# Attention by pairs of heads: values and output projection for two heads at once, low parts in place

## The reference

```
mod = (silu(c) @ wmod).reshape(4, 6, 1, 512)         # shift, scale, gate, twice
h = layernorm(x) * (1 + ca) + sa                     # x: 4 x 512 x 512
q = h @ Wq.T            # 32 heads of 128, rope
k, c_kv = rope part of h @ Wkr.T, h @ Wdk.T          # 8 key/value heads, 4 query heads share one
k, v = c_kv @ Wupk.T, c_kv @ Wupv.T
attn = softmax(causal(q k.T * scale))                # per batch and head, 512 x 512
x = x + ga * ((attn v) @ Wo.T)
h = layernorm(x) * (1 + cb) + sb
w = top8 of softmax(h @ router.T + bias), dense      # 64 experts, each only a bias vector
x = x + gb * (h * sum(w) + w @ expert_bias)
```

## Time and profile before

| what | us |
|---|---|
| median of 3 runs (1528.67 to 1531.39) | 1531.01 |
| the profiled execution | 1527.11 |
| its span | 1525.8 |
| TensorE busy | 1481.6 (97%) |
| VectorE busy | 1167.2 (76%) |
| GpSimd busy | 1079.0 (71%) |
| ScalarE busy | 973.3 (64%) |

### The profile page before, as it was taken

The page is one execution under the profiler, slowest core; times in us unless marked ns, Lnnn a source line. Parts: engine busy times, 40 slices in busy tenths (PEclk is TensorE's granted clock), DMA queues, the critical chain, the costliest instruction groups (busy, mean ns, idle before and its releaser), DMA issues.

```text
span 1525.8 us, 24881 instructions
## 1 busy us (share of the span) xinstructions
PE 1481.6 (97%) x7474; PEld 1264.1 (83%) x7474; DVE 1167.2 (76%) x3441; ACT 973.3 (64%) x2317; POOL 1079.0 (71%) x827
## 2 busy tenths in 40 slices
PE   8979999999999999999999999999999999999976
PEld 4668888888888888888888888888888888888865
DVE  6866777777777777777777777777888899897766
ACT  3356767676676766667666776767566666666663
POOL 1667767676676767767667676766678888886765
PEclk9999999999999999999999999999999999999997
DMA  8547665666656666666666665667778888888750
GB/s 308 211 149 226 203 198 189 207 193 201 197 197 197 197 196 202 203 179 208 199 197 209 201 194 175 215 200 212 220 250 261 260 266 278 268 253 269 247 181 28
DMA packets 210982, 322.03 MB, mean 211 GB/s; under 512 B 38416, under 2 KB 128272, under 8 KB 210848
## 3 DMA queue, kind: packets, MB, share of 16 engines
q1 hardware_dynamic: 210528, 320.33, 66.4%
q10 hardware_dynamic: 320, 0.11, 0.0%
HBM read 179.42 MB, written 140.94 MB: 210 GB/s over the span
## 4 chain that ended last, share of the span: by engine, by line
PE 86%; DVE 5%; POOL 3%; issue 2%; ACT 1%; DMA 1%; SPq 0%; DVEq 0%; POOLq 0%; ACTq 0%
PE bank_s L489 22%; PE bank_o L588 21%; PE bank_pv L573 15%; PE bank_s L538 14%; PE bank_s L512 6%; PE bank_s L500 5%; PE bank_s L468 1%; DMA wmod<-in_wmod 1%; PE bank_o L436 1%; POOL PT_lo L1458 1%; PE bank_s L606 1%; DVE y L1058 1%; DMA blocks<-blocks 0%; POOL rot_c L1446 0%; DVE h_raw L1070 0%
## 5 line engine op out<-in xcount | busy, mean ns | idle before, releaser
L1458 POOL TENSOR_TENSOR PT_lo<-PT_raw,PT_hi 128x640 fp32r<-128x640 f32 x252 | 407.0, 1638 | 91.2 <-ACT PT_hi L839 91.1
L825 ACT ACTIVATE probs<-probs,row_inv 128x512 f32<-128x512 f32 (+3 forms) x512 | 258.8, 554 | 200.5 <-DVE row_inv L1128 200.5
L1446 POOL TENSOR_TENSOR rot_c<-rot_c,rot_s 128x512 f32<-128x512 f32 x128 | 165.7, 1294 | 197.0 <-DVE rot_s L1091 196.8
L818 ACT ACTIVATE probs<-probs,row_min 128x512 f32<-128x512 f32 (+3 forms) x512 | 280.4, 551 | 7.8 <-DVE row_min L1122 7.8
L1451 POOL TENSOR_TENSOR qT_lo<-rot_c,qT_hi 128x512 fp32r<-128x512 f32 x128 | 167.2, 1306 | 92.8 <-ACT qT_hi L800 92.8
L1122 DVE CUSTOM_DVE_ANT_0 probs<-bank_s,mask 128x512 f32<-128x512 f32 (+3 forms) x512 | 231.2, 487 | 1.0 <-issue 0.6
L489 PE MATMUL bank_s<-hT_lo,wq_hi 128*128 128x512 f32 x500 | 205.3, 411 | 5.4 <-issue 3.7
L1145 DVE STREAM_TRANSPOSE blocks<-probs 128x384 f32<-128x384 f32 x508 | 205.2, 442 | 4.1 <-POOL hT_lo L1436 2.1
L588 PE MATMUL bank_o<-wo_lo,OT_hi 128*128 128x512 f32 x504 | 196.7, 390 | 4.2 <-DVE OT_lo L1153 4.2
L588 PE MATMUL bank_o<-wo_hi,OT_lo 128*128 128x512 f32 x504 | 196.5, 390 | 0.0
L588 PE MATMUL bank_o<-wo_hi,OT_hi 128*128 128x512 f32 x504 | 196.3, 390 | 0.0
(11 more groups left out here) (252 smaller groups left out, 3397.6 us busy)
## 6 DMA issues: line engine op xcount, KB each, us to landing
blocks<-blocks SPq DMA_DIRECT2D x127, 640.0 KB, 4.6
PT_raw<-blocks SPq DMA_DIRECT2D x504, 160.0 KB, 3.1
stage<-in_wq SPq DMA_DIRECT2D x32, 256.0 KB, 4.0
vblocks<-kv_raw SPq DMA_DIRECT2D x32, 256.0 KB, 4.3
kv_raw<-vblocks SPq DMA_DIRECT2D x128, 64.0 KB, 2.6
stage<-in_wo SPq DMA_DIRECT2D x32, 256.0 KB, 3.8
split_wq<-wq_hi SPq DMA_DIRECT2D x32, 256.0 KB, 3.6
split_wq<-wq_lo SPq DMA_DIRECT2D x32, 256.0 KB, 3.9
```

Source lines behind the costliest of these rows:

```text
L818: ins = act.activation(row(t, qt), row(t, qt), ACT.Exp, bias=row_min[m][:, qt:qt + 1], scale=-1.0, accum_out=row_sum[m][:, qt:qt + 1])
L825: ins = act.activation(row(t, qt), row(t, qt), ACT.Copy, scale=row_inv[t % 2][:, qt:qt + 1])
L1446: pool.tensor_tensor(rot_c[:], rot_c[:], rot_s[:], ALU.add).then_inc(pool_a, 1)
L1458: pool.tensor_tensor(lo[:, at], raw_of(t)[:, at], hi[:, at].bitcast(F32), ALU.subtract).then_inc(pool_t, 1)
```

## The change

Two heads, `2p` and `2p+1`, form a pair `p`. Their transposed probabilities lie side by side in buffers of twice the size, and one matmul takes columns of both: first the upper two tiles of queries (2 and 3), with key tiles 0 to 3, then the lower two (0 and 1), with key tiles 0 and 1. The output projection goes by pair too, upper tiles in the next odd step and lower tiles in the even step behind it. `PT_raw` and `PT_lo` are one buffer: GpSimd subtracts in place. There is one buffer of values for two. The key and value projections move to `h` = 1 and `h` = 3, the feed-forward pieces to even steps, the weight pieces `wo` one step later. The transposed loads of both heads of a pair are issued in the odd step, when the lower values of the pair before are done. The last two heads go singly as before.

```
-CHUNK_STEP = {0: [0], 1: [1], 2: [2], 3: [3], 5: [4], ...}
+CHUNK_STEP = {1: [0], 2: [1], 3: [2], 4: [3], 5: [4], ...}
-FFN_FROM = (AGAIN - SHARED + 1) * GROUP + 3
+PAIRS = (ALL - 2) // 2
+UPPER, LOWER = (2, 3), (0, 1)
+FFN_FROM = (AGAIN - SHARED + 1) * GROUP + 4
-        PT_hi = whole.take("PT_hi", [P, CAUSAL], F32R)
-        PT = [PT_hi, whole.take("PT_lo", [P, CAUSAL], F32R)]
-        PT_raw = whole.take("PT_raw", [P, CAUSAL])
+        PT_hi = whole.take("PT_hi", [P, 2 * CAUSAL], F32R)
+        PT_raw = Region(whole.at).take("PT_raw", [P, 2 * CAUSAL])
+        PT = [PT_hi, whole.take("PT_lo", [P, 2 * CAUSAL], F32R)]
-        v = [[whole.take(f"v_{p}{i}", [P, QT, HD], F32R) for p in ("hi", "lo")] for i in range(2)]
+        v = [whole.take(f"v_{p}", [P, QT, HD], F32R) for p in ("hi", "lo")]
+        def pair_done(p, tiles):
+            return 2 * p + (1 if tiles == UPPER else 2)
             def scores(...):
-                    if qt == 2 and h == 2 and u + 1 < UNITS:
+                    if qt == 2 and h == 3 and u + 1 < UNITS:
                         pe.wait_ge(dve_kr, u + 2)
-                    if qt == 2 and h == 0 and u > 0:
+                    if qt == 2 and h == 1 and u > 0:
                         pe.wait_ge(dve_vt, u + 1)
+            def values_pair(p, tiles):
+                t = 2 * p
+                pe.wait_ge(pool_t, 2 * (t + 1) + 2)
+                if t % GROUP == 0:
+                    pe.wait_ge(dve_v, t // GROUP + 1)
+                if pair_done(p, tiles) > 1:
+                    pe.wait_ge(dve_o, pair_done(p, tiles) - 1)
+                to = bank["pv"][:].rearrange("p (i k) -> p i k", i=2 * SUBS)
+                last_key = tiles[-1]
+                for kb in range(last_key + 1):
+                    first = max(kb, tiles[0])
+                    at = KEY_OFFSET[kb] // SUBS + (first - kb) * SUB
+                    size = (last_key + 1 - first) * SUB
+                    for n, (a, w) in enumerate(passes(v, PT)):
+                        ps = w[:].rearrange("p (i k) -> p i k", i=2 * SUBS)[:, :, at:at + size]
+                        mm = pe.matmul(to[:, :, (first - tiles[0]) * SUB:], a[:, kb, :], ps, ...)
+                mm.then_inc(pe_pv, 1)
+            def out_pair(p, tiles):
+                pe.wait_ge(dve_o, pair_done(p, tiles))
...
+                for j in tiles:
+                    for h in heads:
+                        o_at = (2 * (j - tiles[0]) + h % 2) * P
+                        for n, (o, w) in enumerate(passes(OT, wo)):
+                            mm = pe.matmul(bank[f"o{j}"][:], o[:, o_at:o_at + P], w[:, h, :], ...)
             def step(t):                                   # TensorE
                 scores(t + 1, QUERY_ORDER, before, n)
+                if h % 2 == 1 and t > 1:
+                    values_pair(t // 2 - 1, LOWER)
                 if t + 3 < ALL:
                     q_proj(t + 3)
-                if h == 0 and u + 1 < UNITS:
+                if h == 1 and u + 1 < UNITS:
                     k_proj(u + 1)
-                if h == 2 and u + 1 < UNITS:
+                if h == 3 and u + 1 < UNITS:
                     v_proj(u + 1)
-                if t >= 2:
-                    out_head(t - 2)
+                if h % 2 == 1 and t > 1:
+                    out_pair(t // 2 - 1, UPPER)
+                if h % 2 == 0 and t > 2:
+                    out_pair(t // 2 - 2, LOWER)
...
-                if 0 < t < ALL - 2:
-                    values(t - 1)
+                if h % 2 == 0 and t > 0:
+                    values_pair(t // 2 - 1, UPPER)
             def step(t):                                   # ScalarE
-                if t >= 2:
-                    o_split_hi(t - 2)
-                if 0 < t < ALL - 2:
+                if h % 2 == 1 and t > 1:
+                    pair_split_hi(t // 2 - 1, UPPER)
+                if h % 2 == 0 and t > 2:
+                    pair_split_hi(t // 2 - 2, LOWER)
+                if h % 2 == 0 and 0 < t < ALL - 2:
                     split_moved_hi(t - 1)
-                if h == 0:
-                    v_split_hi(u)
...
+                if h == 1:
+                    v_split_hi(u)
                 normalise(t + 1, 0)
                 normalise(t + 1, 1)
+                if h % 2 == 1:
+                    split_moved_hi(t - 1)
                 if t + 3 < ALL:
                     q_split(t + 3)
             def step(t):                                   # VectorE
+                if h % 2 == 1 and t > 1:
+                    pair_split_lo(t // 2 - 1, UPPER)
                 mask_and_max(t + 1, 0)
-                if t >= 2:
-                    o_split_lo(t - 2)
+                if h % 2 == 0 and t > 2:
+                    pair_split_lo(t // 2 - 2, LOWER)
                 mask_and_max(t + 1, 1)
...
                 if h == 2 and u > 0:
-                    add_out(u - 1, range(2, QT))
-                if h == 0:
-                    v_split_lo(u)
+                    add_out(u - 1, UPPER)
+                if h == 3 and u > 0:
+                    add_out(u - 1, LOWER)
                 invert_sums(t + 1, 0)
                 if t + 3 < ALL:
                     q_rope(t + 3)
                 invert_sums(t + 1, 1)
-                if h == 0 and u + 1 < UNITS:
+                if h == 1:
+                    v_split_lo(u)
+                if h % 2 == 1:
+                    transpose_blocks(t + 1, QUERY_ORDER[:2])
+                if h == 1 and u + 1 < UNITS:
                     k_rope(u + 1)
-                if h == 2 and u + 1 < UNITS:
+                if h == 3 and u + 1 < UNITS:
                     transpose_values(u + 1)
...
-                if moved(t + 1):
+                if h % 2 == 1:
+                    transpose_blocks(t + 1, QUERY_ORDER[2:])
+                elif moved(t + 1):
                     transpose_blocks(t + 1)
             def step(t):                                   # GpSimd
-                if t > 0:
+                if h % 2 == 0 and t > 0:
                     split_moved_lo(t - 1)
...
                 if t + 3 < ALL:
                     q_rope(t + 3)
+                if h % 2 == 1:
+                    split_moved_lo(t - 1)
+                if t + 3 < ALL:
                     q_split(t + 3)
-                if h == 0 and u + 1 < UNITS:
+                if h == 1 and u + 1 < UNITS:
                     k_rope(u + 1)
             def load_transposed(t):                        # SyncE
-                elif t > 0:
-                    sp.wait_ge(pool_t, 2 * t)
+                elif t > 1:
+                    sp.wait_ge(pe_pv, t // 2 * 2)
             for t in range(ALL):
-                if moved(t):
+                if t % 2 == 1 and moved(t):
+                    load_transposed(t - 1)
                     load_transposed(t)
```

More of the change, by code:

```diff
@@ L240, in build @@
         wdk = [wdk_hi, early.take("wdk_lo", [P, CH, HID], F32R)]
-        assert early.at <= probs_at
+        assert early.at <= blocks_at
         modrow = Region(probs_at).take("modrow", [BATCH, 2, HID])
[L243 to L253, removed]
+        under_blocks = Region(blocks_at)
+        h_raw = [under_blocks.take(f"h_raw{i}", [P, SEQ]) for i in range(2)]
+        c_in = under_blocks.take("c_in", [P, CH, BATCH])
+        c_exp = under_blocks.take("c_exp", [P, CH, BATCH])
+        c_silu = under_blocks.take("c_silu", [P, CH, BATCH])
+        stats = under_blocks.take("stats", [P, QT, 6])
+        mean_var = under_blocks.take("mean_var", [P, TILES, 2])
+        ve = under_blocks.take("ve", [P, TILES])
+        rstd = under_blocks.take("rstd", [P, TILES])
+        power = under_blocks.take("power", [P, TILES])
+        assert under_blocks.at <= probs_at
         assert whole.at <= nc.sbuf_usable_end
@@ L553, in transpose_part @@
                 mm.then_inc(pe_t, 1)
+            def values_pair(p, tiles):
[13 more added lines that the diff above has]
+                        ps = w[:].rearrange("p (i k) -> p i k", i=2 * SUBS)[:, :, at:at + size]
+                        mm = pe.matmul(to[:, :, (first - tiles[0]) * SUB:], a[:, kb, :], ps,
+                                       start=(kb == 0 and n == 0), stop=(kb == last_key and n == 2))
+                mm.then_inc(pe_pv, 1)
@@ new lines, in out_pair @@
+            def out_pair(p, tiles):
+                u = 2 * p // GROUP
+                heads = [2 * p % GROUP, 2 * p % GROUP + 1]
+                pe.wait_ge(dve_o, pair_done(p, tiles))
+                for h in heads:
+                    wait_weights(u, f"wo{h}")
+                if p == 0:
+                    pe.wait_ge(dve_vt, 1)
+                for j in tiles:
+                    if heads[0] == 0 and u > 0:
+                        pe.wait_ge(dve_y, added(u - 1, j))
+                    for h in heads:
+                        o_at = (2 * (j - tiles[0]) + h % 2) * P
+                        for n, (o, w) in enumerate(passes(OT, wo)):
+                            mm = pe.matmul(bank[f"o{j}"][:], o[:, o_at:o_at + P], w[:, h, :],
```

(18 more changed lines are left out.)

132 lines of the change are left out of this document (70 added, 62 removed).

## The result

| | before | after |
|---|---|---|
| median of 4 runs each, us | 1530.95 | 1595.63 |
| range of the runs | 1528.67 to 1531.39 | 1594.98 to 1597.17 |
| span of the profiled execution | 1525.8 | 1593.7 |
| score matmuls of step 4 (start-up ahead of it) | 142.85 | 143.99 |
| steps 4 to 91, 22 shared units | 938.87 (42.68 each) | 967.67 (43.99 each) |

The change makes the kernel slower: ratio 1.0427, interval 1.0409 to 1.0445. The rows of the table under the span are distances between the first score matmuls of steps, the last one from there to the end of the span, and their differences add up to the span's: 1.1 + 28.8 + 33.2 - 0.7 + 5.4 = 67.9 us.

The account below looks back on a forecast made before the run. TensorE, busy 97% of the span, was taken as the bound. Profiled 1527.1 us, plus 29 for 23 shared units and 28 for eight feed-forward units, each net of matmul time saved, made 1584; forecast 1585, range 1525 to 1618.

Parts of the forecast that it names:

- Matmul time removed: TensorE's values product: 18 matmuls a pair for 24, 3.42 us for 3.80, so 0.77 a unit and 24 us off.
- VectorE's chain: Head 1's odd step: key's rotation ends at 12.6, so scores of tile 2 stall TensorE 0.85 us a unit.
- the low part of the values, 1.12 or more: VectorE's new subtraction behind the reciprocal in head 1's odd step, taken as 1.12 us or more, ending at 9.3.
- GpSimd's chain: Second head's low part ends 8.5 us into head 2's even step, delaying upper values; with the rotation's wait 1.3 us.
- Head 2's lower values: Lower values due at 24.1 wait for VectorE, ending at 24.6 behind ScalarE's late copy, and start at 24.75: 0.65 us.
- Sum of a shared unit: Stalls 1.3 + 0.65 + 0.1 less 0.77 saved: +1.3 us, bounds -0.77 and +2; 23 units, +29 us.
- Feed-forward units: Eight units carrying feed-forward work: stalls of 4.3 us, net +3.5 a unit, 28 us in all; bounds +1.2 and +5.2.
- Cost nothing, with 1 us of cover: Transposed loads of a pair: first head lands at about 7.8, second at 9.5, wanted at 8.9 and 12.2.
- The end: The tail, where a pair's output work moves ahead of the last wait: nothing, bounds +-2.7 us.
- TensorE's 24 us come through whole: Faster rival: both chains, VectorE's rotation and GpSimd's low part, stay hidden, giving 1507 us; chance 0.14.
- Only the rotation waits: Rival: only the key's rotation stalls TensorE, GpSimd's chain being 1 us shorter: 6 us, 1535 (1528 to 1545); chance 0.15.
- Loads land late: Rival: paired loads come in bursts and delay GpSimd and the upper values; 1 us late is 63 us, 1648; chance 0.13.

Follow-up runs that it names:

- the by-head runs: Values' matmuls one head at a time, 36 a pair for 18: in the changed kernel 1624.58 us (ratio 1.0639), in the 1519.28 us version 1551.19 us (1.0139).
- The run with the rotation's wait taken away: Changed kernel with VectorE making the low part of the values ahead of the query's rope, not behind it: 1594.59 us, ratio 1.0436.
- the fastest version: Changed kernel with three orders mended, store behind loads, gating behind query's low part, GpSimd's statistics and VectorE's last feed-forward operation earlier: 1519.28 us, ratio 0.9936.
- the orders were mended: Changed kernel with VectorE's, GpSimd's and ScalarE's orders altered, SyncE's store behind the loads, and feed-forward operations of GpSimd and VectorE moved: 1519.28 us, ratio 0.9936.
- mending all: Changed kernel with low part of the values early, GpSimd's weight piece behind, and ScalarE's upper-values and feed-forward copies ahead, together: 1557.28 us, ratio 1.0184.

## Why the prediction was right, and where its terms were off

**The total and its sign.** 1595.6 for 1585, within 1525 to 1618, by the mechanism forecast: the removed matmul time is real, and waits in the written order of VectorE and GpSimd give back more. The range is wide and held a rival too. The 10.6 us over the forecast come from the feed-forward units and the end, not from the shared units.

**Matmul time removed: right.** 3.42 predicted; measured 2.42 and 1.10, of which 0.07 is the restart: 3.45. By the formula of the Trainium skill (TensorE: Matmul & The Clock Gate, "Back-to-back issue gap"), columns over the clock and 2.5 ns for each matmul, the by-head runs would be an estimated 3 us slower; they were about 30 slower. The prediction used this formula where it isn't meant: the section gives it for an isolated gap, and says that in a stream of weight loads and matmuls both set the spacing, with about 131 ns for 512 columns. That figure doesn't hold here either, as 512 columns took 227 ns.

**VectorE's chain: the mis-sized term.** The prediction let the key's rotation end at 12.6 and TensorE stall for 0.85, 0.95 with the restart. The rotation ended at 13.05 (694.23, the odd step having begun at 681.18); the tile started 1.24 late, and the scores as a whole took 1.58 more. The term at fault is "the low part of the values, 1.12 or more": it took 1.80, in each of the 22 shared units. A second, smaller term stood in no step of the walk: the query projection's wait for the mask, 0.22. The 1.12 came from one row; I did not ask what GpSimd did beside it. Here GpSimd's sum of the query's rope (689.28 to 690.57) starts 0.04 ahead of it; the subtraction ended at 691.12, 0.55 after the sum. Without a neighbour it takes 0.69, as the run with the subtraction ahead shows. The trace of the kernel before held the same: in 6 of its 22 shared units the subtraction took 1.84 or 1.85, as it met an instruction of GpSimd just begun. The row of 1.12 began 1.00 behind the start of one, and GpSimd's next one was then 0.45 longer:

```profile
743.49 1.85 DVE L1111 TENSOR_TENSOR v_lo<-kv_raw,v_hi 128x512 fp32r<-128x512 f32 x1
```
```profile
699.93 1.58 POOL L1458 TENSOR_TENSOR PT_lo<-PT_raw,PT_hi 128x640 fp32r<-128x640 f32 x1
701.46 2.03 POOL L1458 TENSOR_TENSOR PT_lo<-PT_raw,PT_hi 128x640 fp32r<-128x640 f32 x1
...
743.22 1.58 POOL L1458 TENSOR_TENSOR PT_lo<-PT_raw,PT_hi 128x640 fp32r<-128x640 f32 x1
```

The Trainium skill (SBUF — State Buffer, "Who interferes with whom") states the rule that I should have used: a VectorE instruction with two SBUF inputs and a GpSimd instruction that reads SBUF exclude each other, and the later one waits. The trace agrees: 1.80 us in the 31 places beside GpSimd's sum, 0.69 in the one place without it. The low part of the output (L1231), which reads one of its inputs from PSUM, kept its 0.69 beside GpSimd.

**GpSimd's chain: exact, and hidden.** 8.5 into the even step predicted, 8.51 measured. But the stall before it was larger than forecast, so TensorE came at 8.97 and found the low part done. So one stall of 1.58 stands for the two that were to cost 1.3 together. The run with the rotation's wait taken away showed this chain right behind it.

**Head 2's lower values: 0.65 predicted, 0.36 measured** (0.19 of idle and a slower restart). VectorE ended at 705.80, 24.6 after the odd step's start as forecast; TensorE came at 24.4 for the 24.1 that I had, again by the larger first stall.

**Sum of a shared unit: +1.3 predicted, 43.99 - 42.68 = +1.3 measured**, with terms of 1.58 and 0.36 instead of 1.3, 0.65 and 0.1. The first was 0.3 too small and the second 0.3 too large. That isn't all luck: VectorE's end at 24.6 sets where TensorE goes on, and a larger first stall leaves a smaller second one. That 24.6 came out although the rotation's chain did not is due to GpSimd's chain, which sets it.

**Feed-forward units: +3.5 a unit predicted, 33.2 / 7 = +4.7 measured**, within the bounds (1.2 to 5.2). Two causes stood in no step of the walk. ScalarE's copy of the transposed tile (L924) stood behind the query's copy, and score tiles waited for it (7.6 us); what this costs no run shows by itself. And the loads, "Cost nothing, with 1 us of cover", had in these steps a store ahead of them that waits for GpSimd: moving it gave 7.8 us by itself. The cover was counted for the transfers, not for SyncE's queue.

**The end: nothing +-2.7 predicted, +5.4 measured.** In step 126, where no query projection is left, the output product of the lower tiles waits; TensorE and ScalarE:

```profile
1539.17 0.63 PE L613 MATMUL bank_o<-wo_lo,OT_hi 128*128 128x512 f32 x1 [2.89 <-DVE OT_lo L1231]
1539.60 0.63 PE L613 MATMUL bank_o<-wo_hi,OT_lo 128*128 128x512 f32 x1
...
1542.92 0.39 PE L613 MATMUL bank_o<-wo_lo,OT_hi 128*128 128x512 f32 x1
...
1544.76 0.50 PE L595 MATMUL bank_pv<-PT_lo,v_hi 128*128 128x512 f32 x1 [0.98 <-POOL PT_lo L1551]
```
```profile
1536.55 1.36 ACT L902 ACTIVATE PT_hi<-PT_raw 128x640 fp32r<-128x640 f32 x2 [1.03 <-DMA PT_raw<-blocks]
1537.82 0.58 ACT L912 ACTIVATE OT_hi<-bank_pv 128x512 fp32r<-128x512 f32 x1
```

ScalarE waited for the pair's load, and the copy that TensorE needs stands behind it. That idle of 2.89 is 1.4 more than the one before the change (1.45); behind it the granted clock was at its lower level, 1.2 GHz: eight matmuls at 0.43 us from start to start and one at 0.33 instead of 0.23, 1.7 us. The upper values (2.55), which now stand here, and their wait (0.98) follow. From step 126 on there are 18 matmuls more than before the change (12 of the output, 6 of the values); that work stood ahead of step 4 before. From the first of these output matmuls to the transposes of the last heads it is 8.1 us for 3.75 before (1475.24 to 1478.99), from there to the end 0.4 less: 1.4 + 4.4 - 0.4 = 5.4. This is read from the trace and not shown by a run; the fastest version still pays 6.3 there, with 6.8 us at the lower clock in it, from 1463.0 on.

**The rivals.** "TensorE's 24 us come through whole" failed in the changed kernel, and less than half of it came true when the orders were mended: 10 us of the 24 in all (0.0064 of 1529). "Only the rotation waits" held in what is seen (one wait of over 1 us a unit), not in its time, since the GpSimd chain was no shorter. "Loads land late" was false in the shared units and true in part with feed-forward.

## What to carry to other kernels

When two waits end close together, an experiment on one can show next to nothing (three of them, none told from the change by its ratio), and mending all shows what they cost (37 us). Before calling a wait harmless, take away the others too. In a kernel whose busiest engine is at 97%, merging its instructions pays only what the written order of the others lets through. Move the engines' work with the steps, each queue by itself, SyncE's too. And take an operation's duration together with what its neighbours do at that time: the same subtraction cost 0.69, 1.12 or 1.80 us. And look at the granted clock of a stretch before comparing its length with that of another run.

## What the runs showed of the hardware

The VectorE subtraction of two SBUF operands of 128 x 512 took 0.69 us alone and 1.80 when it began 0.04 behind a GpSimd sum, which kept its 1.29. Before the change it met GpSimd's low part: begun 0.27 behind an instruction of 1.58 it took 1.85; begun 1.00 behind one it took 1.12, and GpSimd's next instruction took 2.03 for 1.58. In all these rows it ended 0.54 to 0.55 us after the GpSimd instruction that was ahead of it. Small matmuls that each bring new weights cost 0.115 to 0.119 us from start to start with 256 columns or a mix of 256 and 128, and 0.227 with 512. An idle time of 2.89 us, to 1539.17, was followed by a stretch at the lower clock. The first row below has that idle in it. One of 2.71 us in the kernel before, to 1466.67, had the full clock behind it (1.00 from 1466 to 1472); so the length of one idle time does not decide it, and what does is not shown here. The rows:

```profile
1533.00:1539.00 6.00, 3.29 (x19) 2.78 (x17) 4.36 (x14) 4.96 (x12) 1.64 (x2) 1.00 1.04 261
1539.00:1542.50 3.50, 3.33 (x8) 2.63 (x9) 2.54 (x11) 3.50 (x12) 3.50 (x3) 0.56 0.85 302
1543.00:1547.00 4.00, 3.02 (x14) 2.15 (x13) 0.69 (x1) 0.64 (x2) 3.92 (x4) 1.00 0.85 254
```
